# A gated delta rule over 16 key heads: block inverse kept in half its width, decayed k and q made chunk by chunk, conv ops and output work reordered

## The reference, cut to what matters

```python
mixed = hidden_states @ W_qkv
conv = sum((xp[:, i:i + T, :] * conv_w[:, i] for i in range(KC)))      # KC = 4 taps
mixed = _silu(conv)
q, k, v = split(mixed)              # 16 key heads of 128; 32 value heads of 128, two per key head
def step(S, xs):
    qt, kt, vt, gt, bt = xs
    S = S * jnp.exp(gt)[..., None, None]
    kS = jnp.einsum('bhk,bhkv->bhv', kt, S)
    S = S + bt[..., None, None] * kt[..., :, None] * (vt - kS)[..., None, :]
    o = jnp.einsum('bhk,bhkv->bhv', qt, S)
    return (S, o)
o = o * rsqrt(mean(o * o) + 1e-06) * norm_w * _silu(z)
y = o @ W_out
```

## Time and profile before

| | |
|---|---|
| median of 3 runs | 2123.1 us (2117.54 to 2123.35) |
| the profiled execution | 2117.74 us, its span 2115.8 us |
| loop over key heads | starts at 708.95 us, 16 turns |
| a turn | 86.83 us (the first 85.26) |
| mean granted clock of PE | 0.976 |

### The profile page before, as it was taken

How to read it: one execution, slowest core, us unless ns; L and a number is a source line. 1 busy time by engine, 2 the same in 40 slices (tenths; PEclk the granted TensorE clock), 3 DMA queues, 4 the chain that set the end, 5 groups by cost and what they waited for, 6 DMA issues and landing times.

```text
span 2115.8 us, 43478 instructions
## 1 busy us (share of the span) xinstructions
PE 1917.6 (91%) x15082; PEld 1402.3 (66%) x15082; DVE 1505.7 (71%) x2430; ACT 984.2 (47%) x2535; POOL 759.0 (36%) x685
## 2 busy tenths in 40 slices
PE   4578886888799999999999999999999999999998
PEld 3246662333555687877878778787687777877877
DVE  5786771111677687787787877878778787787887
ACT  1012224777213354645545455455564555645544
POOL 4730002110300334616336164362543624526343
PEclk9689998999899999999999999999999999999999
DMA  6635661000122200010010000100001001010010
GB/s 245 209 91 200 184 178 55 26 20 1 55 60 70 82 17 35 5 35 30 15 35 10 30 30 15 35 30 10 30 15 35 30 10 40 5 35 30 15 45 20
DMA packets 75254, 111.75 MB, mean 53 GB/s; under 512 B 23318, under 2 KB 56742, under 8 KB 72006
## 3 DMA queue, kind: packets, MB, share of 16 engines
q1 hardware_dynamic: 71694, 102.32, 15.1%
q0 software_dynamic: 3072, 8.39, 1.3%
q10 hardware_dynamic: 446, 0.48, 0.1%
HBM read 85.80 MB, written 28.52 MB: 54 GB/s over the span
## 4 chain that ended last, share of the span: by engine, by line
PE 51%; DVE 16%; issue 4%; ACT 3%; POOL 0%; DVEq 0%; ACTq 0%; POOLq 0%
PE ps L1273 5%; PE ps L1311 4%; PE ps L1321 4%; DVE conv L1862 3%; DVE P L2034 3%; DVE P_term L2031 3%; PE ps L1544 3%; PE ps L1493 3%; PE ps L1533 3%; PE ps L1428 3%; PE ps L1417 3%; PE ps L1546 3%; PE ps L1520 2%; PE ps L1450 2%; PE ps L1525 2%
## 5 line engine op out<-in xcount | busy, mean ns | idle before, releaser
L1862 DVE SCALAR_TENSOR_TENSOR conv<-raw,tap_st,conv 128x1024 f32<-128x1024 f32 x204 | 299.5, 1468 | 3.6
L1273 PE MATMUL ps<-xnT,w_conv_st 128*128 128x512 f32 x544 | 247.6, 599 | 0.0
L1842 POOL TENSOR_TENSOR o<-o,silu_z 128x256 f32<-128x256 f32 x128 | 138.5, 1082 | 255.5 <-DVE silu_z L1882 141.7
L816 DVE TENSOR_REDUCE m_part<-ps 128x1 f32<-128x640 f32 (+7 forms) x176 | 176.4, 1027 | 67.1 <-PE ps L667 53.5
L1726 POOL TENSOR_TENSOR gmask_Q<-upto,g 128x2048 f32<-128x2048 f32 x17 | 61.4, 3611 | 363.5 <-PE ps L1500 335.5
L998 ACT ACTIVATE probs<-ps 128x1024 f32<-128x1024 f32 (+7 forms) x256 | 145.9, 660 | 58.1 <-PE ps L933 28.7
L1273 PEld LDWEIGHTS ps<-xnT,w_conv_st 128*128 128x128 f32 x544 | 98.9, 191 | 101.1 <-issue 96.2
L1565 ACT COPY raw<-ps 128x512 f32<-128x512 f32 x136 | 80.7, 594 | 173.4 <-PE ps L1273 173.4
L1822 POOL TENSOR_TENSOR kq_decayed<-conv,decay_rows 128x1024 f32<-128x1024 f32 x64 | 159.3, 2521 | 0.0
L1321 PE MATMUL ps<-w_z_st,xnT 128*128 128x256 f32 x512 | 148.8, 393 | 0.0
L903 POOL DMA_INDIRECT slot_outputs<-scratch_slots_y,token_slots x32 | 30.6, 958 | 310.9 <-POOLq L496 202.0
(11 more groups left out here) (345 smaller groups left out, 4728.9 us busy)
## 6 DMA issues: line engine op xcount, KB each, us to landing
decay_rows<-scratch_egc SPq DMA_DIRECT2D x17, 1024.0 KB, 4.7
w_conv_st<-in_w_conv SPq DMA_DIRECT2D x17, 512.0 KB, 3.3
scratch_slots_x<-yacc SPq DMA_DIRECT2D x8, 1024.0 KB, 14.9
slot_rows<-scratch_slots_x SPq DMA_DIRECT2D x16, 512.0 KB, 4.7
scratch_slots_y<-slot_outputs SPq DMA_DIRECT2D x16, 512.0 KB, 3.4
w_gate_up<-in_gu SPq DMA_DIRECT2D x8, 768.0 KB
w_gate_up<-in_gu SPq DMA_DIRECT2D x32, 192.0 KB
kq_decayed<-in_gu SPq DMA_DIRECT2D x22, 256.0 KB, 2.8
```

Of the source, the lines that this page charges most:

```text
L816: dve.tensor_reduce(dst, src, AX.X, ALU.max).then_inc(s_max, 1)
L1273: mm = pe.matmul(ps[:, 6 + n % 2, :], wc[:, k, (n // 2) * P:(n // 2 + 1) * P], m.xnT[:, k, (n % 2) * HALF:(n % 2 + 1) * HALF], start=k == ...
L1842: g.tensor_tensor(oc, oc, zs[:, c, :], ALU.mult).then_inc(s_oz, 1)
L1862: op = dve.scalar_tensor_tensor(out=cv[:, t, :], in0=raw[:, t, at:at + T], scalar=tap[:, t, at:at + 1], in1=cv[:, t, :], op0=ALU.mult, op1 ...
```

## The change

- After the inverse of the 16x16 blocks, P and Q are kept as 64 columns per unit instead of 128 (`pd`, `qd`, two halves of the old `gm_q`), since each half of the rows has its values in its own 64 columns. Two chunks are turned by one transpose. X and QX of the two levels move 32 columns instead of 64; in level 5 `place` puts chunks of even number into the low and of odd number into the high half of the rows. ACT copies a turned tile by four copies over half the rows each where the places change.
- Decayed k and q are made by POOL for one chunk at a time (`decayed`), as soon as the running head's chunk has been used in the recurrence; the one for the last chunk after it. `gmask` of the next head now also waits for its second conv tile. The decay rows are loaded at the start of a turn.
- Conv: five instead of four ops ahead of level 4, two in level 4, three in level 5, one ahead of the recurrence, six in it; the last three are done at the start of the next turn, two of them ahead of the U products.
- Output turns and projections, the additions to y and the gating of outputs take other places in the first stage. U's diagonal blocks are copied to PSUM, the identity start of `pc` is done by ACT, and `uc` is made by a reduction.
- The experts' buffers lie in other tiles, constants for the narrower masks are added, and the masks of unused levels are dropped.

The number of projections ahead of the turns of the spread blocks (`for n in range(5): project(i + 1, n)`) is 5 before and after.

```diff
+def place(lv, c, h):
+
+    j, hi = c // 2, int(h is HI)
+    if lv == FIRST:
+        return h, c, 0, c, 0, c
+    return (LO, HI)[c % 2], 2 * j + hi, hi, j, c % 2, j
+
+def halves(e):
+
+    turned = ps[:, 2 + e, :].rearrange("p (j h n) -> p j h n", h=2, n=64)
+    return [(h, odd, turned[(LO, HI)[odd], :, int(h is HI), :]) for h in (HI, LO) for odd in range(2)]
+
+def base(lv, e):
+
+    return (e, (4, 0)[e], (4, 1)[e])[lv - FIRST]
...
+sp.wait_ge(s_kqe, i * 7 + 7)
+decay_rows(m.egc_rows[bass.ds(2 * i + 2, 2), :])
...
-sp.wait_ge(s_kqe, i * 4 + 4)
-decay_rows(m.egc_rows[bass.ds(2 * i + 2, 2), :])
...
 for b in range(4):
+    if b == 2:
+        pe.wait_ge(s_e, i * 4 + 4)
+        for n in range(2):
+            turn_outputs(i, n)
     for c in (2 * b, 2 * b + 1):
         mm = pe.matmul(ps[:, 4 + b, (c % 2) * 256:(c % 2 + 1) * 256], cv[:, 1, c * P:(c + 1) * P],
                        cv[:, 0:2, c * P:(c + 1) * P], start=True, stop=True)
     mm.then_inc(s_kk, 1)
-pe.wait_ge(s_e, i * 4 + 4)
-for n in range(4):
+for n in range(2):
+    project_out(i, n)
+for n in range(2, 4):
     turn_outputs(i, n)
-for n in range(3):
...
-pe.wait_ge(s_cvd, i * 4 + 4)
+pe.wait_ge(s_cvd, i * 4 + 3)
 pe.wait_ge(s_u, i * 4 + 4)
 turn_v(0, 6)
-project_out(i, 3)
+for n in range(2, 4):
+    project_out(i, n)
...
-    for c in range(NC):
-        mm = pe.transpose(ps[:, 2 * e + c // 4, (c % 4) * P:(c % 4 + 1) * P], e_p[:, e, c, :], m.ident[:])
+    for j in range(NC // 2):
+        mm = pe.transpose(ps[:, 2 + e, j * P:(j + 1) * P], pd[:, e, 2 * j:2 * j + 2, :].rearrange("p c n -> p (c n)"), m.ident[:])
...
+                g, at, bank, slot, _, _ = place(lv, c, h)
+                dst = ps[g, bank + base(lv, e), slot * 32:(slot + 1) * 32].rearrange("p (b s) -> p b s", s=s)
+                mm = pe.matmul(dst, ua[h, e, c, 1, h], qd[h, e, c, :].rearrange("p (b t s) -> p b t s", t=2, s=s)[:, :, 0, :],
...
+                g, at, _, _, bank, slot = place(lv, c, h)
+                mm = pe.matmul(ps[h, bank + base(lv, e), slot * 32:(slot + 1) * 32], pd[g, e, at, :], xs32[g, e, at, :], start=True, stop=True)
...
-pe.wait_ge(s_pt, i * ND + NT)
...
-for n in range(4):
+tanh_conv(i, 3)
+for n in range(2):
     turn_out(i, n)
+nc.scalar.copy(pc[:], eye1[:].unsqueeze(1).broadcast_to([P, UNITS, BLK])).then_inc(s_ch, 1)
...
+    nc.scalar.copy(ps[rows, U_BANK, :].rearrange("p (u n) -> p u n", u=UNITS), uu[rows, :, rows]).then_inc(s_u32, 1)
+for n in range(2, 4):
+    turn_out(i, n)
 act.wait_ge(s_rk, i * 5 + 1)
-act.wait_ge(s_ch, i * SUBS)
...
-    nc.scalar.copy(chunks(gm_q[:, e]), two_banks(2 * e)).then_inc(s_q, 1)
+    for h, odd, src in halves(e):
+        last = nc.scalar.copy(qd[h, e, odd::2, :], src)
+    last.then_inc(s_q, 1)
...
-    nc.scalar.copy(chunks(e_p[:, e]), two_banks(2 + 2 * e)).then_inc(s_pt, 1)
+    if lv == FIRST:
+        nc.scalar.copy(chunks(pd[:, e]), ps[:, 2 + e, :]).then_inc(s_pt, 1)
+    else:
+        for h, odd, src in halves(e):
+            last = nc.scalar.copy(e_p[h, e, odd::2, h], src)
+        last.then_inc(s_pt, 1)
+tanh_conv(i + 1, 1)
...
+def decayed(c):
+
+    at = slice(c * P, (c + 1) * P)
+    for e in range(2):
+        op = g.tensor_tensor(kqe[:, e, :, at], cv[:, 0:2, at], egr[:, e, at].unsqueeze(1).broadcast_to([P, 2, P]), ALU.mult)
+    op.then_inc(s_kqe, 1)
...
-pool.wait_ge(s_egr, i * 16 + 16)
+pool.wait_ge(s_conv, i * 4 + 4)
 passed()
-for e in range(2):
-    for a in range(2):
-        g.tensor_tensor(kqe[:, e, a, :], cv[:, a, :], egr[:, e, :], ALU.mult).then_inc(s_kqe, 1)
...
 pool.wait_ge(s_x, i * ND + ND)
+pool.wait_ge(s_cvd, i * 4 + 6)
 gmask(i + 1)
...
+pool.wait_ge(s_egr, i * 16 + 32)
+for c in range(1, NC):
+    if c < NC - 1:
+        pool.wait_ge(s_su, i * 14 + 2 * c + 1)
+    else:
+        pool.wait_ge(s_aw, i * NC + NC)
+    passed()
+    decayed(c)
+    if c == 6:
         pool.wait_ge(s_vn, i * 2 + 2)
         pool.wait_ge(s_hm, i * 3 + 3)
         scalars(i + 1)
-    pool.wait_ge(s_var, i * 16 + 2 * c + 2)
...
+    gate_z(c - 1)
+    if c == 4:
+        rsqrt_outputs(i, 0)
+gate_z(NC - 1)
+rsqrt_outputs(i, 1)
+totals(i + 1)
...
-gate_outputs(i, 1)
+for k in range(2, TAPS):
+    conv_op(i, 3, k)
...
-for n in range(3):
-    add_out(i, n)
+gate_outputs(i, 1)
+conv_op(i, 3, TAPS)
+add_out(i, 0)
 dve.wait_ge(s_u32, i * 5 + 4)
 dve.wait_ge(s_hm, i * 3 + 2)
-dve.tensor_tensor(u32[:], u32[:], hm[:].unsqueeze(3).broadcast_to([P, UNITS, 2, BLK]), ALU.mult).then_inc(s_um, 1)
+dve.tensor_tensor(u32[:], ps[:, U_BANK, :].rearrange("p (u t i) -> p u t i", t=2, i=BLK),
+                  hm[:].unsqueeze(3).broadcast_to([P, UNITS, 2, BLK]), ALU.mult).then_inc(s_um, 1)
 dve.wait_ge(s_um, i + 1)
-dve.tensor_tensor(uc[:], u32[:, :, 0, :], u32[:, :, 1, :], ALU.add).then_inc(s_uc, 1)
-add_out(i, 3)
+dve.tensor_reduce(uc[:], u32[:].rearrange("p u t i -> p u i t"), AX.X, ALU.add).then_inc(s_uc, 1)
+for n in range(1, 4):
+    add_out(i, n)
 n = 1
-dve.tensor_copy(pc[:], eye1[:].unsqueeze(1).broadcast_to([P, UNITS, BLK])).then_inc(s_ch, 1)
 for k in range(BLK - 1):
...
 todo = ([(0, k) for k in range(TAPS)] + [(1, 0), (0, TAPS)] + [(1, k) for k in range(1, TAPS)]
-        + [(1, TAPS)] + [(2, k) for k in range(TAPS)] + [(3, 0), (3, 1), (2, TAPS), (3, 2), (3, 3), (3, TAPS)])
+        + [(2, 0), (1, TAPS), (2, 1), (2, 2), (2, 3), (3, 0), (2, TAPS), (3, 1)])
 def more(n=1):
     for _ in range(n):
         if todo:
             conv_op(i + 1, *todo.pop(0))
-dve.wait_ge(s_kqe, i * 4 + 4)
-more(4)
+dve.wait_ge(s_kqe, i * 7 + 7)
+more(5)
 for lv in range(FIRST, LEVELS - 1):
     s, n0 = 1 << lv, 2 * (lv - FIRST)
     for e in range(2):
...
-    more(3)
...
+    more(2 + lv - FIRST)
 for e in range(2):
     dve.wait_ge(s_x, i * ND + NT + e + 1)
-    dve.tensor_copy(xs[HI, e], ps[HI, e, :].rearrange("p (c n) -> p c n", c=NC)).then_inc(s_xt, 1)
...
+    dve.tensor_copy(xs[HI, e], ps[HI, base(LEVELS - 1, e), :].rearrange("p (c n) -> p c n", c=NC)).then_inc(s_xt, 1)
+more(1)
 silu_z(i, 0)
-more(1)
...
-more(1)
 assert not todo
...
```

More of the change, by code:

```diff
@@ L619, in _ @@
             step.link(g.memset(m.lmask[:], 1.0))
-            for lv in range(LEVELS):
-                s = 1 << lv
-                ap = m.lmask[:, lv, :].rearrange("p (b s) -> p b s", s=s)
+            for n in range(2):
+                s = 1 << (FIRST + n)
+                ap = m.lmask[:, n, :].rearrange("p (b s) -> p b s", s=s)
                 step.link(g.affine_select(out=ap, in_=ap, compare_op=ALU.is_ge, fill=0.0, base=-s,
@@ L1485, in _ @@
                             for h in (LO, HI):
-                                mm = pe.matmul(ps[h, e, c * 64:(c + 1) * 64], e_p[h, e, c, h], xs[h, e, c, :], start=True, stop=True)
+                                g, at, _, _, bank, slot = place(lv, c, h)
+                                mm = pe.matmul(ps[h, bank + base(lv, e), slot * 32:(slot + 1) * 32], pd[g, e, at, :], xs32[g, e, at, :], start=True, stop=True)
                         mm.then_inc(s_y, 1)
@@ L1491, in _ @@
                         pe.wait_ge(s_yt, i * NT + n0 + e + 1)
-                        for c in range(NC):
-                            mm = pe.transpose(ps[:, 2 + 2 * e + c // 4, (c % 4) * P:(c % 4 + 1) * P], gm_q[:, e, c, :], m.ident[:])
+                        for j in range(NC // 2):
+                            mm = pe.transpose(ps[:, 2 + e, j * P:(j + 1) * P], qd[:, e, 2 * j:2 * j + 2, :].rearrange("p c n -> p (c n)"), m.ident[:])
                         mm.then_inc(s_t, 1)
@@ L1499, in _ @@
                     for c in range(NC):
-                        mm = pe.matmul(ps[HI, e, c * 64:(c + 1) * 64], ua[LO, e, c, 1, HI], gm_q[LO, e, c, LO], start=True, stop=True)
+                        mm = pe.matmul(ps[HI, base(LEVELS - 1, e), c * 64:(c + 1) * 64], ua[LO, e, c, 1, HI], qd[LO, e, c, :], start=True, stop=True)
                     mm.then_inc(s_x, 1)
-                pe.wait_ge(s_pt, i * ND + NT)
                 project_z(i, 0)
@@ L1508, in _ @@
                     for c in range(NC):
-                        mm = pe.matmul(ps[LO, e, c * 64:(c + 1) * 64], xs[HI, e, c, :], e_p[HI, e, c, HI], start=True, stop=True)
+                        mm = pe.matmul(ps[LO, base(LEVELS - 1, e), c * 64:(c + 1) * 64], xs[HI, e, c, :], e_p[HI, e, c, HI], start=True, stop=True)
                     mm.then_inc(s_y, 1)
@@ L1514, in _ @@
                 pe.wait_ge(s_pt, i * ND + ND)
+                pe.wait_ge(s_kqe, i * 7 + 7)
                 for c in range(NC):
@@ L1795, in _ @@
             totals(0)
-            pool.wait_ge(s_conv, 4)
+            pool.wait_ge(s_cvd, 2)
+            pool.wait_ge(s_egr, 16)
             passed()
-            g.tensor_copy(tap[:], m.taps[:, 1]).then_inc(s_taps, 1)
-            pool.wait_ge(s_dve, 5)
+            for c in range(1, NC):
+                decayed(c)
+            pool.wait_ge(s_dve, 7)
             passed()
@@ L1962, in _ @@
```

(2 more changed lines are left out.)

111 lines of the change are left out of this document (61 added, 50 removed).

## The result

The changed kernel takes 2046.3 us (median of four runs, 2044.4 to 2047.9), the kernel before 2123.2 (2117.5 to 2124.1). The profiled execution has a span of 2043.7 us, 72.1 less than that of the kernel before.

What follows compares the result with a forecast made beforehand. TensorE, busy 91%, was taken to bound the kernel, its small idle times being waits for other engines. Terms summed to -2.3 us a turn, -37 over sixteen, +2 outside, giving 2085 us after half the runs' spread; range 2050 to 2119.

Steps and rivals of the forecast that it cites:

- level 5's term: Level 5, 6.81 to 5.9 us: transposes -0.9, 0.65 wait mostly gone, -0.3 of tails, but +0.9 for products placed otherwise.
- all paired: Level 5's QX if every matmul pass runs beside a partner: 0.93 us per e; X the same.
- none paired: Level 5's QX if no pass has a partner: 1.9 us per e; X the same; the term assumed 1.4 for QX.
- the upper bound: Level 5's QX wholly serial by the skill's rule, the turn 0.9 us worse.
- Rival 3: Better than forecast: all pairs run, chunk 0's conv op precedes gmask, or 32-column passes cost less; 2040 to 2071; chance 0.22.
- Rival 1: Level 5's products don't pair: 2.8 us a turn lost against a gain of 2.3, ending slower at 2130; chance 0.13.
- First stage: Start of a turn, 19.16 us: PE's wait at spread matmuls L1450 goes whole, kq ops moved out among the reasons; -1.0.
- Rival 4: POOL late at the head, held up by DVE's conv ops; the 1.0 us wait stays or doubles; 2101 to 2117; chance 0.10.
- Turns, level 4, level 6: P turns halved, -0.7; level 4 transposes halved and DVE ops narrower, -1.7; X copies late in level 6, +0.45.
- The recurrence: 27.42 us: later gmask on POOL slows chunk 0's conv op, so KS of chunk 1 waits on PE; +1.55.
- Rival 2: POOL's decayed k and q push conv ops in the chunks: 0.35 us in six chunks, 2.1 a turn; 2119; chance 0.12.
- Outside the loop: MoE conv work 0; at the end POOL's last decayed chunk and a z gate precede the root, +2 us.

## Why the prediction was wrong

**The step that failed** is level 5's term, -0.9 us. The new places of its products stood there as a loss of 0.9 us, with X paired and QX half paired, between the bounds "all paired" and "none paired". The trace of before held only two placements, two quadrants and one, and I read them as "a partner or none", two passes at most at a time. The runs show another form: one pass per 0.058 us in each quadrant, and four quadrants at once. The placement was a gain of 1.61 us (5.18 us against 3.57, only the places, their banks and ACT's copies for them differ), so this part of the term had the wrong sign and was off by 2.5 us a turn; that is shown from both levels and by the order of issue. The transposes and the masks, the rest of the term, had been taken 0.2 us too high. Over 16 turns the term's error is 37 us; the prediction was off by 39.

The Trainium skill, "TensorE: Matmul & The Clock Gate", section on packing small matmuls, says that a weight load overlaps matmuls in flight only where the row group differs; it stood beside the upper bound. The trace disagrees with it here: QX's neighbours in level 5 share their rows and differ in their columns, and they run at once (64 passes in 1.14 us).

**Rival 3** had the sign and, with 2040 to 2071, the time; but of its three mechanisms only the first (all pairs run) stands near what happened, and it was priced at 0.9 instead of 2.5. That the time fell into its stretch is luck for the most part. The other two were refuted: the conv op of chunk 0 did not get in before gmask, and 32 columns took as long as 64 (2.06 and 2.08 us in level 4), as the earlier trace rows had suggested. **Rival 1** had the opposite of the truth.

**First stage.** The wait at the spread matmuls went whole, as forecast. But of the reasons that the forecast gave for it, the kq ops were not needed: with them back in the head the spread matmuls still wait for nothing, because the mask (0.68 us) and the new form of the sum (0.70 instead of 2.46) aren't slowed beside POOL. What the kq ops cost the head is 0.50 us at the output turns. So about 0.85 of the 1.36 us come from the other edits of this stage, which no run takes apart. The 0.36 us beyond the forecast are small waits of PE, most of them at the first output projection of before (two gaps, 0.3 us in all, too short to show as idle time). In the next stage the forecast had nothing, and 0.38 us went: a wait for P before its first turn (the turn at 1174.55 came 0.28 us later than the pace of the fifth projection's passes allowed) and a first group without a slow start (4.17 against 4.28). Rival 4 did not come.

**Turns, level 4, level 6.** -0.67, -1.61 and +0.41 against -0.7, -1.7 and +0.45. The halved transposes, the narrower DVE ops and the copies of X that come late (0.37 us idle behind L2143) are right.

**The recurrence.** +1.69 against +1.55, at the place and for the cause named: the conv op behind gmask, 4.51 us, KS idle for 1.80. The runs without it show its price, 1.85 us a turn. Rival 2 is refuted: POOL's busy time in the recurrence rose from 12.2 to 19.4 us, and S to S stayed at 3.67.
The Trainium skill, "SBUF — State Buffer", section "SBUF: two separate sides", calls the port pair that DVE and POOL share an exclusive lock for a whole instruction. The trace agrees (4.51 us for a conv op of 1.28 beside a gmask of 3.61). Yet the meetings in the chunks cost PE nothing: a conv op of 1.66 instead of 1.28 us at most left DVE 0.3 us before the next S, and the gating of outputs in chunk 6, 1.75 instead of 1.23, just ended ahead of it.

**Outside the loop.** The tail grew by 2.9 us, forecast +2. The start of the loop, 3.9 us later in the profile, isn't the change's so far as can be seen: the seven profiles of kernels with the same program ahead of the loop put it between 708.5 and 714.4 us, and before's is 709.0. With one conv op fewer ahead of the loop it was at 717.6, with the decay rows' DMA back in its old place at 717.0, which doesn't blame the DMA either. What moves it stays open.

**The sum.** 15 x 5.16 + 1.5 in the first turn = 78.9, less 3.9 and 2.9, is the 72.1 us between the spans.

## What to carry to other kernels

Here small matmuls ran at once when each had a quadrant of its own, so count quadrants, not partners, and issue them in turn; a copy that moves half the data to the other row half can pay for itself. When the trace holds only two placements, a third is not bounded by them: put the rate that all resources would give into the range. A DVE op that is slowed beside POOL belongs in a slot where its engine would wait anyway, or can be written in a form that isn't slowed, as the sum of U was. And a stall of under 2 us on PE can be followed by a lower clock that costs as much again.

## What the hardware showed that was not expected

- 64 fp32 passes of 64x64 took 2.06 us in two quadrants and 1.14 us in four; 32 in one quadrant took 2.08. The same pace per quadrant, a pass every 0.058 us, for 32 and for 64 columns.
- With eight passes of one quadrant in a row, the next quadrant's run started 0.26 us after it: passes start ahead of up to three that were issued earlier.
- A 1.67 us wait of PE was followed by a granted clock of 0.5 in two of three otherwise equal turns, which cost 1.66 or 2.86 us; the 1.80 us wait ahead of chunk 1 in the changed kernel left it at 1.00.
- Beside the kq ops on POOL, the mask of U from PSUM took 0.68 us and its sum as a reduction 0.70, while the sum of two SBUF halves took 2.46 us in the kernel before.
